# Three additions of 512 columns move from VectorE to GpSimd in a pipelined four-layer graph kernel

## What is computed

```python
# x, adj: (32, 256, 256); every line for each of the 32 graphs
def L0(x, adj, W):
    agg = einsum('bij,bjf->bif', adj, x) / maximum(sum(adj, -1, keepdims=True), 1e-6)
    return relu(einsum('bnf,of->bno', concatenate([x, agg], 2), W))
def gcn(x, adj, W, b):
    return einsum('bnm,bmh->bnh', adj, einsum('bnf,fh->bnh', x, W)) + b
def L1(x, adj, W1, b1, W2, b2, W3, b3):
    return gcn(relu(gcn(relu(gcn(x, adj, W1, b1)), adj, W2, b2)), adj, W3, b3)
def L2(x, mask, adj, dist, W_qkv, W_out, b_out):      # 8 heads of 64, dist is adj
    dots = where(m2, q @ k.T / 8, -big)               # m2: mask of rows and columns
    attn = 0.33 * softmax(dots) + 0.33 * where(m2, adj, 0) + 0.33 * exp(-where(m2, dist, big))
    return (attn @ v) @ W_out + b_out
def L3(x, adj, W_qk, W_v):                            # q, k: 64 columns each
    w = softmax(sum((q @ k.T / 8) * adj, -1, keepdims=True), axis=1)
    return w * (x @ W_v.T)
x = layernorm(x + L0(x, adj, W))
x = layernorm(x + L1(x, adj, ...))
x = layernorm(x + L2(x, nodemask, adj, adj, ...))
x = layernorm(x + L3(x, adj, W_qk, W_v))
```

## Time and profile before

| | us |
|---|---|
| median of 3 runs | 1298.9 (1297.4 to 1299.2) |
| the profiled execution | 1298.5, of it span 1296.7 |
| PE busy | 1272.6 (98%) |
| DVE busy | 1194.8 (92%) |
| ACT busy | 910.6 (70%) |
| POOL busy | 140.7 (11%) |

### The profile page before, as it was taken

How to read it: one execution, slowest core, us unless ns; L and a number is a source line. 1 busy time by engine, 2 the same in 40 slices (tenths; PEclk the granted TensorE clock), 3 DMA queues, 4 the chain that set the end, 5 groups by cost and what they waited for, 6 DMA issues and landing times.

```text
span 1296.7 us, 30200 instructions
## 1 busy us (share of the span) xinstructions
PE 1272.6 (98%) x10848; PEld 1162.8 (90%) x10848; DVE 1194.8 (92%) x3789; ACT 910.6 (70%) x2445; POOL 140.7 (11%) x265
## 2 busy tenths in 40 slices
PE   7999999999999999999999999999999999999997
PEld 6899999999898999898999999998989998989986
DVE  6988999999999999999999999999999999999996
ACT  7677767677667677667677676776676776776773
POOL 0100111101111101111101111011111011110011
PEclk9999999999999999999999999999999999999999
DMA  6110111110111110111100111101111101110000
GB/s 227 34 35 2 35 43 43 43 43 3 42 43 43 43 42 2 43 43 43 43 24 20 43 43 43 43 3 43 43 43 43 32 12 43 43 43 9 10 10 25
DMA packets 34306, 49.00 MB, mean 38 GB/s; under 512 B 7920, under 2 KB 16880, under 8 KB 34160
## 3 DMA queue, kind: packets, MB, share of 16 engines
q1 hardware_dynamic: 34160, 47.08, 11.6%
HBM read 38.68 MB, written 8.39 MB: 36 GB/s over the span
## 4 chain that ended last, share of the span: by engine, by line
PE 75%; DVE 17%; issue 4%; ACT 2%; DMA 1%; POOL 0%; SPq 0%; DVEq 0%; POOLq 0%
PE psum L1485 57%; PE psum L1499 6%; PE psum L1735 5%; PE psum L1693 5%; DVE x L901 3%; DVE work L1030 3%; DVE x_pre L959 2%; DVE bn L867 2%; DVE x_pre L1114 2%; DVE x_pre L969 1%; DVE qkT_l L838 1%; DVE x2T_l L838 1%; PE psum L1786 1%; ACT self_part L385 1%; PE psum L1789 1%
## 5 line engine op out<-in xcount | busy, mean ns | idle before, releaser
L534 ACT ACTIVATE work<-work,shift 128x256 f32<-128x256 f32 x512 | 253.6, 498 | 37.8 <-DVE shift L1030 37.8
L1049 DVE SCALAR_TENSOR_TENSOR work<-work,rsum,extra 128x256 f32<-128x256 f32 x512 | 216.6, 474 | 0.1
L1030 DVE CUSTOM_DVE_ANT_0 work<-psum,minus_big 128x256 f32<-128x256 f32 x512 | 189.3, 415 | 1.9 <-PE psum L1693 1.9
L385 ACT ACTIVATE work<-psum 128x512 f32<-128x512 f32 x256 | 138.1, 595 | 73.5 <-PE psum L1499 69.6
L385 ACT ACTIVATE sup_h<-psum 128x512 fp32r<-128x512 f32 x124 | 73.3, 591 | 144.4 <-PE psum L1485 144.2
L342 POOL TENSOR_TENSOR mv<-mv,eps 128x2 f32<-128x2 f32 x128 | 33.3, 260 | 1141.9 <-DVE mv L888 1141.9
L1485 PE MATMUL psum<-x2T_h,wqkv_h 128*128 128x256 f32 x512 | 146.4, 286 | 5.7 <-DVE x2T_l L838 5.5
L1485 PE MATMUL psum<-x2T_l,wqkv_h 128*128 128x256 f32 x512 | 143.1, 279 | 0.0
L1485 PE MATMUL psum<-x2T_h,wqkv_l 128*128 128x256 f32 x512 | 143.1, 279 | 0.0
L1499 PE MATMUL psum<-ident,work 128*128 128x128 f32 x1024 | 129.0, 274 | 0.0
L1735 PE MATMUL psum<-work,v_sb 128*64 128x256 f32 x1024 | 124.6, 385 | 0.0
(11 more groups left out here) (182 smaller groups left out, 3720.1 us busy)
## 6 DMA issues: line engine op xcount, KB each, us to landing
xT_sb<-in_xT SPq DMA_DIRECT2D x32, 256.0 KB, 2.7
adjT_sb<-in_adjT SPq DMA_DIRECT2D x32, 256.0 KB, 3.0
adj_sb<-in_adj SPq DMA_DIRECT2D x32, 256.0 KB, 4.6
x_sb<-in_x SPq DMA_DIRECT2D x32, 256.0 KB, 4.8
out<-y_sb SPq DMA_DIRECT2D x32, 256.0 KB, 4.5
work<-in_wqkv SPq DMA_DIRECT2D x1, 1536.0 KB, 10.6
mask_row<-in_nodemask SPq DMA_DIRECT2D x32, 32.0 KB, 4.5
w_raw<-in_w SPq DMA_DIRECT2D x3, 256.0 KB, 6.1
```

Of the source, the lines that this page charges most:

```text
L385: return nc.scalar.activation(dst, src, ACT.Copy, scale=scale)
L534: last = nc.scalar.activation(prob[:, p % 2, i, h], prob[:, p % 2, i, h], ACT.Exp, bias=shift[:, p % 2, h, i:i + 1], scale=-1.0, accum_out ...
L1030: last = V_.tensor_tensor_reduce(out=prob[:, p % 2, i, h], in0=bank(SCORES[p] + h)[:, i * N:(i + 1) * N], in1=minus_big[:, g % 2, i], scal ...
L1049: last = V_.scalar_tensor_tensor(out=prob[:, p % 2, i, h], in0=prob[:, p % 2, i, h], scalar=rsum[:, p % 2, h, i:i + 1], in1=extra[:, g % 2 ...
```

## The change

The three additions are made by GpSimd, each with a semaphore that GpSimd increments (pool_x1_b3, pool_x2_bout, pool_adj_sum), and leave DVE's lists. DVE's `gcn_out`, `attention_out` and `adj_extra` and SP's loads wait for these. Since x1 and x2 are now read by another engine, `norm_apply(0)` and `norm_apply(1)` wait until the addition of the graph before is done; GpSimd waits for x1, x2 and exp_adj, and for the readers of its output buffers. In the code of after, the removed DVE calls were not replaced, and in GpSimd's list `norm_rstd(1, 3)` now stands ahead of `norm_rstd(2, 1)`; nothing else changed its order.

```diff
             def load(g):
-                reuse(sp, dve_adj_sum, once(g - 2))
+                reuse(sp, pool_adj_sum, once(g - 2))
...
+            def adj_sum(g):
+                if not live(g):
+                    return
+                pool.wait_ge(act_exp_adj, once(g))
+                nc.gpsimd.tensor_tensor(exp_adj[:, :, :], exp_adj[:, :, :], adj_sb[:, g % 2], ALU.add) \
+                    .then_inc(pool_adj_sum, 1)
+
+            def bias_sum(dst, src, row):
+                return nc.gpsimd.tensor_tensor(dst, src, row[:, :].unsqueeze(1).broadcast_to([P, NT, F]), ALU.add)
+
+            def x1_bias(g):
+                if not live(g):
+                    return
+                if g == 0:
+                    pool.wait_ge(dma_biases, 16 * BIAS_DMAS)
+                pool.wait_ge(dve_x[0], once(g))
+                reuse(pool, dve_x2_pre, once(g - 1))
+                bias_sum(x1_b3[:, :, :], x1[:, :, :], b3_row).then_inc(pool_x1_b3, 1)
+
+            def x2_bias(g):
+                if not live(g):
+                    return
+                pool.wait_ge(dve_x[1], once(g))
+                reuse(pool, dve_x3_pre, once(g - 2))
+                bias_sum(x2_bout[:, g % 2], x2[:, :, :], bout_row).then_inc(pool_x2_bout, 1)
+
             def slot(s):
                 norm_rstd(3, s - 4)
+                x1_bias(s)
+                adj_sum(s + 1)
                 norm_rstd(1, s)
                 norm_rstd(2, s - 2)
                 norm_rstd(0, s + 1)
+                x2_bias(s)
 
             def first_graphs():
                 norm_rstd(0, 0)
+                adj_sum(0)
+                x1_bias(0)
                 norm_rstd(0, 1)
                 norm_rstd(1, 0)
+                adj_sum(1)
+                x1_bias(1)
+                x2_bias(0)
                 norm_rstd(0, 2)
                 norm_rstd(1, 1)
+                adj_sum(2)
+                x2_bias(1)
+                x1_bias(2)
+                adj_sum(3)
                 norm_rstd(1, 2)
...
             def norm_apply(k, g):
                 dve.wait_ge(pool_rstd[k], once(g))
+                if k == 0:
+                    reuse(dve, pool_x1_b3, once(g - 1))
+                if k == 1:
+                    reuse(dve, pool_x2_bout, once(g - 1))
...
-            def adj_sum(g):
-            def x1_bias(g):
-            def x2_bias(g):
...
             def adj_extra(g):
-                dve.wait_ge(dve_adj_sum, once(g))
+                dve.wait_ge(pool_adj_sum, once(g))
...
             def gcn_out(g):
                 dve.wait_ge(pe_gcn, once(g))
+                dve.wait_ge(pool_x1_b3, once(g))
...
             def attention_out(g):
                 dve.wait_ge(pe_y, once(g))
-                dve.wait_ge(dve_x2_bout, once(g))
+                dve.wait_ge(pool_x2_bout, once(g))
...
             def slot(s):
-                x1_bias(s - 3)
...
-                adj_sum(s - 2)
...
-                x2_bias(s - 3)
```

More of the change, by code:

```diff
@@ L187, in graph_blocks_kernel @@
         dma_xT, dma_adjT = sems("dma_xT"), sems("dma_adjT")
-        pool_const, pool_ident = sem("pool_const"), sem("pool_ident")
+        pool_const, pool_ident, pool_x1_b3, pool_x2_bout, pool_adj_sum = (
+            sem(n) for n in ("pool_const", "pool_ident", "pool_x1_b3", "pool_x2_bout", "pool_adj_sum"))
         pool_var, pool_rstd = sems("pool_var", 4), sems("pool_rstd", 4)
@@ L205, in graph_blocks_kernel @@
         act_sup, act_hid, act_hid_hi = sems("act_sup", 3), sems("act_hid"), sems("act_hid_hi")
-        (dve_w, dve_xT, dve_adjT, dve_deg, dve_rdeg, dve_adj_sum, dve_extra, dve_sup0, dve_agg, dve_x1_pre,
-         dve_x1_b3, dve_x1_lo, dve_x2_pre, dve_x2_bout, dve_x2T, dve_qk, dve_scores, dve_rsum, dve_prob, dve_oT,
+        (dve_w, dve_xT, dve_adjT, dve_deg, dve_rdeg, dve_extra, dve_sup0, dve_agg, dve_x1_pre,
+         dve_x1_lo, dve_x2_pre, dve_x2T, dve_qk, dve_scores, dve_rsum, dve_prob, dve_oT,
          dve_x3_pre, dve_x3T, dve_k3_hi, dve_k3, dve_gate,
          dve_gate_shift, dve_gate_rsum, dve_gate_prob, dve_x4_pre, dve_y) = (
-            sem(n) for n in ("dve_w", "dve_xT", "dve_adjT", "dve_deg", "dve_rdeg", "dve_adj_sum", "dve_extra",
-                             "dve_sup0", "dve_agg", "dve_x1_pre", "dve_x1_b3", "dve_x1_lo", "dve_x2_pre",
-                             "dve_x2_bout", "dve_x2T", "dve_qk", "dve_scores", "dve_rsum", "dve_prob", "dve_oT",
+            sem(n) for n in ("dve_w", "dve_xT", "dve_adjT", "dve_deg", "dve_rdeg", "dve_extra",
+                             "dve_sup0", "dve_agg", "dve_x1_pre", "dve_x1_lo", "dve_x2_pre", "dve_x2T", "dve_qk", "dve_scores", "dve_rsum", "dve_prob", "dve_oT",
                              "dve_x3_pre", "dve_x3T", "dve_k3_hi", "dve_k3", "dve_gate", "dve_gate_shift",
@@ L362, in first_graphs @@
                 norm_rstd(0, 3)
+                x2_bias(2)
+                x1_bias(3)
+                adj_sum(4)
+                norm_rstd(1, 3)
                 norm_rstd(2, 1)
-                norm_rstd(1, 3)
                 norm_rstd(0, 4)
+                x2_bias(3)
                 norm_rstd(3, 0)
+                x1_bias(4)
+                adj_sum(5)
                 norm_rstd(1, 4)
@@ L369, in first_graphs @@
                 norm_rstd(0, 5)
+                x2_bias(4)
             def last_graphs():
@@ L1198, in first_graphs @@
                 adj_lo(1)
-                adj_sum(0)
                 norm_apply(0, 0)
@@ L1205, in first_graphs @@
                 sup0_lo(1)
-                x1_bias(0)
                 sup_lo(0, 0)
@@ L1228, in first_graphs @@
                 degrees(2)
-                adj_sum(1)
                 sup_lo(0, 1)
@@ L1240, in first_graphs @@
                 scores(0, 0, 1)
-                x1_bias(1)
                 scores(0, 1, 0)
@@ L1251, in first_graphs @@
                 qk_lo(0, 2)
-                x2_bias(0)
                 hidden_lo(1, 1)
@@ L1271, in first_graphs @@
                 x2_lo(1)
-                x2_bias(1)
                 out_lo(0, 0)
@@ L1280, in first_graphs @@
                 probs(0, 3, 1)
-                adj_sum(2)
                 qk_lo(1, 1)
@@ L1298, in last_graphs @@
                 recip_sums(G - 3, 0)
-                x1_bias(G - 2)
                 probs(G - 3, 0, 0)
@@ L1334, in last_graphs @@
                 x3_lo(G - 4)
-                adj_sum(G - 1)
-                x2_bias(G - 2)
                 norm_stats(3, G - 5)
@@ L1349, in last_graphs @@
                 qk_lo(G - 2, 1)
-                x1_bias(G - 1)
                 tail_gate(G - 4)
@@ L1444, in last_graphs @@
                 gate_maximum(G - 2)
-                x2_bias(G - 1)
                 norm_apply(3, G - 3)
```

10 lines of the change are left out of this document (removed).

## The result

| | before | after |
|---|---|---|
| median of 4 runs, us | 1299.05 (1297.4 to 1299.6) | 1309.8 (1308.4 to 1310.7) |
| the profiled execution, us | 1298.5, span 1296.7 | 1310.0, span 1308.2 |

The ratio is 1.0084, interval 1.0066 to 1.0101: 10.8 us slower, where 1317 us were forecast.

A forecast was written before the change was run, and what follows sets the result against it. PE was taken to set the pace except in one DVE stretch from aggregate to x2T_l. 1298.5 + 15 (hold) + 2.4 (start) + 1 (end) = 1316.9, so 1317 us, with a range of 1297.5 to 1334.

The forecast's parts named there:

- The removal, 0 us: Three additions per graph, 1.8 us, leave DVE outside its pace-setting stretch and only lengthen its waits: 0 us.
- The addition, 1.3 us: One 512-column addition on GpSimd takes 1.3 us, between bounds of 0.65 and 1.74 us.
- DVE is held, by an addition that came first: At norm_apply(0), DVE waits on the shared read path until GpSimd's earlier x2_bias is nearly over: 15 us in all.
- DVE keeps its turn: Rival: DVE is never held, or the addition ends before norm_apply(0); 1298.5 us, not slower; chance 0.22.
- Long additions: Rival: GpSimd additions take 1.74 us, lengthening the holds by x2_bias and adj_sum; 1341 us; chance 0.08.
- the freed time reaches PE: Rival: DVE's pace-setting stretch shrinks by the 0.44 us that PE idles per graph; 1286 us; chance 0.06.
- The size of the hold, 0.51 us: x2_bias holds norm_apply(0), ahead of x2T_l, 0.51 us in each of 28 steady slots; 15 us taken.
- adj_sum, 0 us and near the edge: adj_sum holds hidden_lo and DVE 0.9 to 1.1 us per graph, covered by 1.21 us of slack: 0 us.
- The start, +2.4 us: Both norm_apply pairs of graph 0 may wait for adj_sum(0) and adj_sum(1), 1.2 us each.
- The end, +1 us: In last_graphs norm_apply(2) stands ahead of norm_mean(0), so x2_bias holds its pair 1.2 us once.
- The large term: x2_bias's steady hold of norm_apply(0), 0.51 us over 28 slots: 15 us taken.
- the small one: The start's holds of graph 0's two norm_apply pairs: +2.4 us.

The follow-up runs named there:

- e2: Kernel before with only x1_bias and adj_sum moved to GpSimd, x2_bias staying on DVE; median 1303.9 us, ratio 1.0047.
- e3: Kernel after with x2_bias placed later in GpSimd's list, behind the next norm_rstd(3); median 1303.6 us, ratio 1.0043.
- e4: Kernel before plus one idle GpSimd addition at x2_bias's place in each steady slot, no other engine waiting for it; median 1306.7 us, ratio 1.0066.
- e6: Kernel after with x2_lo put ahead of norm_apply(0) in DVE's steady list; median 1305.1 us, ratio 1.0054.
- e10: Kernel before plus two idle GpSimd additions in a row at x2_bias's place in each steady slot; median 1334.6 us, ratio 1.0282.
- e7: Kernel before plus a GpSimd memset of 1280 columns at x2_bias's place in each steady slot; median 1300.8 us, ratio 1.0026.

## Why the prediction was right, and which terms were off

- **The removal, 0 us: right.** e2 and e3 run their steady parts within 1.4 us of before's with two and three additions gone. The time went where it was said: these waits of after (total us, times, longest) are the longer for it, the first from 24.2 us in before, the second from 1.9.

```profile
DVE oT_l L883 <- ACT oT_h L430: 42.0, 36, 1.5
...
DVE work L1058 <- PE psum L1706: 16.8, 30, 1.0
```

- **The addition, 1.3 us: right.** 1.28 us unhindered. The Trainium skill, GPSIMD Engine Reference, section Performance versus the Vector engine, led to an estimate of 1.12; the trace is 14% above it.
- **DVE is held, by an addition that came first: right.** That was the step that no row showed, and e4 shows it bare. So the rival *DVE keeps its turn* (1298.5) falls. *Long additions* falls with 1.28 us, and *the freed time reaches PE* with e2 and e3.
- **The size of the hold, 0.51 us: mis-sized, it is 0.24.** x2_bias started 5.59 - (619.45 - 614.64) = 0.78 us ahead of norm_apply, not 0.66: it followed its power at 618.75 + 0.74 by -0.04, not by +0.08. And DVE goes on earlier than I had it: 620.23 + 0.24 = 620.47, which is 0.25 us before the addition's end at 620.72. I had taken 0.13 from a power on two columns, where the other engine yields; e4 gives 0.25 as well (618.82 - 618.57). 1.27 - 0.78 - 0.25 = 0.24. The Trainium skill, SBUF — State Buffer, section Who interferes with whom, has the pair held for the whole instruction; the trace agrees on the turns and gives 0.25 us less. With 0.24 the term would have been 28 x 0.24 = 7 instead of 15; it came as 6. For the same reason PE's wait is 0.68 us and not 0.95, and the period 39.60 and not 39.9.
- **adj_sum, 0 us and near the edge: right**, by another victim: not hidden_lo but the degree operation ahead of it, held 1.1 us of 1.21 at hand.
- **The start, +2.4 us: too small, it is +4.7** (+5.6 from graph 0 to 3, less 0.8 ahead of it). I charged both norm pairs one addition each. The first pair and adj_extra(0), which reads exp_adj and masks in SBUF, are held for 1.95 us, of which some 0.8 arrives. The second pair is held by two additions, which costs 1.7. Graph 1's pair is held by adj_sum(2), which costs most of 1.0, though I had written that the other steps of the start had waits on both sides, without following the new list past its first two additions. The last 1.3 is the half clock, of which the prediction had nothing.
- **The end, +1 us: right**, +0.7.

Sum: 4.7 + 6.1 + 0.7 = 11.5, for a forecast of 18.4. The large term was over twice too large and the small one half of what it was, so it is luck that the total looks better than its parts. The way the time went, and where, was right for its reasons.

**What stays open.** Why TensorE's clock drops at the start in some executions and not in others with as much idling; why DVE goes on 0.25 us before an addition's end in one place and 0.14 in the other; and how the 0.8 us ahead of gcn_out(0) divides between the first two holds and what wanders there.

## What to carry to other kernels

- Before an elementwise step goes to GpSimd, look for what DVE does in the 1.3 us after its start, not for how busy either engine is. If that is an operation with both data inputs in SBUF or a TENSOR_SCALAR, and DVE sets the pace there, the move costs time even when it takes work off DVE.
- A stretch in which an engine is never idle has to be followed to its real end, through every semaphore that the other engine waits for. Reordering inside it renames the wait, and gains only where it moves an operation out from under GpSimd's (e6); find the stretch by its constant length, as 8.29 us here.
- The hand-written start deserves the same walk through as the loop: four holds there cost some 3.4 us, over half as much as 28 in the steady part, and how much of a hold arrives depends on what else the chain waits for.

## What the runs showed of the hardware that I had not expected

- A TENSOR_SCALAR of 128x2 elements is held like one of 128x256: 155 ns alone, 1254 ns behind an addition.
- DVE goes on about 0.25 us before the end of GpSimd's record, in after, e4 and e10 alike (in e10 the second half has its usual 0.40 us from 626.39, and the additions end at 626.65). The degree operation goes on only 0.14 us before (604.34 + 1.25 - 0.15 = 605.44, and adj_sum ends at 605.58).
- A memset, which reads nothing, holds DVE's TENSOR_SCALAR pair too, by the 0.10 us that its length gives.
- The granted clock fell to 0.50 for 3.4 or 6.8 us near 19 to 26 and at 43 us in several executions, two that start as before does among them (e4 and e7). At 43 us it cost 1.3 us.
